# Earlier norms and first products, and one paired comparison on VectorE, in the front of a fused graph and expert kernel

## The chip, the cores and the metric

One core of one Trainium2 chip. The metric is the device time of one execution in microseconds (us). The kernel before takes 1289.39 us, the median of three runs (1287.55 to 1292.88).

## The reference, cut to what matters

Four blocks follow each other on 1250 tokens of 512 numbers: a graph network of three layers, experts, a second graph block with attention, and a last feed-forward block with top-k choices. The change touches only the start of the first:

```
h = _layernorm(x)
for l in range(3):
    neigh = jax.ops.segment_sum(h[src], dst, num_segments=n) * inv_deg
    h = h @ Ws_self[l] + neigh @ Ws_neigh[l] + bs[l]
    if l != 2: h = relu(h)
x = x + h
```

There are 40000 edges (src, dst), sorted by dst.

## The kernel before

The 1250 tokens are 10 tiles of 125. The kernel never gathers rows: it counts the edges into a matrix `adj` (source against target token), and `segment_sum` becomes a matrix product with it. The front, about the first 140 us, builds `adj` and beside it the first layer's products.

**Counting.** The edges lie in 80 *runs* of 4 x 125. For each of the four groups of a run, one matmul of TensorE (line 2397) multiplies a 125 x 125 matrix of ones that marks each edge's source within its tile (`hot_lo`, stationary) by a matrix that marks tile and target (`hot_key`, moving, 80 to 400 columns: 10 tiles times a window of 8 to 40 targets that grows with the run), all in bf16, summed in PSUM. VectorE then adds the window into `adj` (line 1686). Runs 0 to 78 are written out; a small loop does the last one.

Who makes the ones of run t: the first two rows of `hot_lo` (three from run 60 on, where the window is 36 or more; `lo_by_act`) come from ScalarE by a square (line 1050) and a relu for all of them (line 1058). The others come from VectorE, a `tensor_scalar` comparison each (line 1668). `hot_key` is VectorE's: below run `PAIRED` = 60 in one `tensor_tensor` comparison for all four groups (line 1672), on fp16 numbers that lie in pairs (`key_pairs`, `key16`), from run 60 on by four `tensor_scalar` (line 1677). All buffers of ones are double.

**Norms and products.** Beside the runs each tile of x is normed and turned, and the turned tile is multiplied by the layer's two matrices: 80 matmuls of 512 columns in 32 bits (line 2067; each shows as two records), here called products. For tile i: moments on VectorE (line 506, 508), square root on ScalarE (512), reciprocal (516) and normed rows (521) on VectorE, four transposes on TensorE (526), and a copy to `hT` on ScalarE (532). Later ScalarE copies the high part of a tile's neighbour product (line 894, `act_z_hi`, here "z copy") and the self product (938, 939, `act_self`, "self copy"), and VectorE takes the rest (1262, `vec_z`).

**What sets the order.** Each engine has its own program, written out by hand: a loop over a step t, in which `every(t, first, gap)` says that tile i's part stands in step first + gap x i. `FIRST_LN` and `FIRST_Z` are the two starting points, and TensorE issues products up to `products_to(t)`, 8 in 7 runs:

```
def products_to(t):
    return min(max(0, (t - FIRST_Z) * 8 // Z_GAP), 8 * NT - KD)
```

Each engine does its instructions in order. In step t ScalarE makes the squares of run t, then the ones of run t-1, then the norms' and products' parts of step t. VectorE makes the ones and keys of run t, adds run t-2, then its parts. TensorE turns a tile ahead of run t's counts and does products behind them. ScalarE's table of functions must be loaded anew for the square root (once). x comes in two halves by SP's queue (lines 677, 680); the products' weights are line 678.

## Time and profile before

| | us |
|---|---|
| median of 3 runs | 1289.39 |
| the profiled execution, its own time | 1294.25 |
| its span | 1292.5 |
| TensorE busy in the span | 1221.8 |
| VectorE busy | 550.1 |
| ScalarE busy | 452.1 |
| run 0's counts begin | 15.72 |
| the counts of run 78 are added | 139.43 |

The profile is of one execution. A busy TensorE is not TensorE at its peak, since matmuls are pipelined and their ends are modelled; a start is better evidence than an end. In a timeline the bracket behind a row says how long the engine was idle before it and which engine's instruction released it.

### The profile page before, as it was taken

The page shows a single profiled execution, that of the slowest core. Times are in us where ns is not written, and L with a number is a line of the kernel's source. Part 1 is how long each engine was busy: PE and PEld are TensorE (multiplying, and loading weights), DVE is VectorE, ACT ScalarE, POOL GpSimd, SP SyncE. Part 2 cuts the span into 40 slices and gives each one's busy share as a digit, 9 for nine tenths or more (in the row PEclk, how much of TensorE's full clock was granted, in tenths as well). Part 3 has the DMA queues.
Part 4 walks back from the last instruction along what each step waited for, and adds up shares of the span by engine and source line. Part 5 has one row for each costly group of instructions (what it writes and reads, how often), then busy time and mean ns, then how long its engine had stood idle before and what let it go on. Part 6 is the DMA issues. An engine that isn't in the chain of part 4 may idle for free. (4 is left out here: it accounts for less than half of the span.)

```text
span 1292.5 us, 19378 instructions
## 1 busy us (share of the span) xinstructions
PE 1221.8 (95%) x6528; PEld 817.9 (63%) x6529; DVE 550.1 (43%) x1535; ACT 452.1 (35%) x965; POOL 227.9 (18%) x227
## 2 busy tenths in 40 slices
PE   4999899999999899999999999999989999989797
PEld 3555485467458455488787887777465586564465
DVE  8999643333444343100000000001485345675773
ACT  7878533233223300011111111111112343338872
POOL 1000070030000028201111111111453000116530
PEclk9999999999999889999999999999988999999899
DMA  9200000000012300761166114456452000200011
GB/s 225 86 1 1 1 2 1 0 2 2 0 57 82 124 1 1 243 240 49 45 235 247 48 42 167 151 209 231 121 145 87 3 32 2 74 0 1 1 34 48
DMA packets 42978, 98.25 MB, mean 76 GB/s; under 512 B 4142, under 2 KB 6632, under 8 KB 41874
## 3 DMA queue, kind: packets, MB, share of 16 engines
q1 hardware_dynamic: 28642, 68.70, 15.9%
q0 software_dynamic: 6144, 16.45, 4.7%
q10 hardware_dynamic: 8112, 12.08, 2.6%
q8 instruction: 45, 0.74, 0.2%
q14 instruction: 35, 0.29, 0.1%
HBM read 81.02 MB, written 16.17 MB: 75 GB/s over the span
## 5 line engine op out<-in xcount | busy, mean ns | idle before, releaser
L498 PEld LDWEIGHTS psum<-sb_blk,sb_w_reg 128*128 128x128 f32 x1792 | 204.0, 192 | 12.8 <-issue 12.8
L498 PE MATMUL psum<-sb_blk,sb_w_reg 128*128 128x128 f32 x1792 | 205.2, 275 | 1.7 <-issue 1.7
L2145 PE MATMUL psum<-sb_z_reg_r,sb_hT_conv_r 125*125 125x512 f32 x385 | 157.0, 408 | 0.4 <-DVE sb_z_last L1262 0.4
L1434 DVE TENSOR_TENSOR sb_blk<-sb_blk,psum 128x256 f32<-128x256 f32 x56 | 23.6, 421 | 277.0 <-ACT sb_blk L955 277.0
L498 PE MATMUL psum<-sb_hT_conv,sb_w_reg 128*128 128x416 f32 (+3 forms) x336 | 110.0, 485 | 4.8 <-issue 4.8
L2145 PE MATMUL psum<-sb_htok_r,sb_hT_conv_r 125*125 125x512 f32 x285 | 112.9, 396 | 0.0
L2235 PE MATMUL psum<-sb_w_reg,sb_blk 128*128 128x512 f32 x224 | 100.8, 592 | 0.0
L498 PEld LDWEIGHTS psum<-sb_hT_conv,sb_w_reg 128*128 128x128 f32 x336 | 67.2, 204 | 42.2 <-issue 38.2
L2145 PEld LDWEIGHTS psum<-sb_z_reg_r,sb_hT_conv_r 125*125 125x125 f32 x385 | 72.0, 187 | 18.0 <-issue 0.7
L2067 PE MATMUL psum<-sb_w_reg,sb_hT_conv 128*125 128x512 f32 x160 | 81.8, 605 | 0.0
L955 ACT ACTIVATE sb_blk<-psum 128x256 f32<-128x256 f32 x56 | 21.5, 384 | 163.9 <-PE psum L498 163.9
L905 ACT CAST sb_hT_conv_r<-sb_a_reg 125x625 fp32r<-125x625 f32 x80 | 56.2, 717 | 54.7 <-PE psum L2145 50.7
L2397 PEld LDWEIGHTS psum<-sb_hT_conv,sb_sil 125*125 125x125 bf16 x316 | 37.7, 145 | 52.5 <-issue 23.4
L2235 PEld LDWEIGHTS psum<-sb_w_reg,sb_blk 128*128 128x128 f32 x224 | 40.4, 190 | 40.2 <-issue 40.2
L2397 PE MATMUL psum<-sb_hT_conv,sb_sil 125*125 125x80 bf16 (+7 forms) x316 | 49.6, 282 | 14.4 <-ACT sb_sil L1058 7.0
L2145 PEld LDWEIGHTS psum<-sb_htok_r,sb_hT_conv_r 125*125 125x125 f32 x285 | 53.5, 188 | 12.6 <-issue 0.5
L1050 ACT ACTIVATE sb_blk<-sb_sil,sb_blk 125x125 bf16<-125x125 f16 x177 | 59.9, 394 | 1.8 <-DVE sb_blk L1622 0.5
L2118 PE MATMUL psum<-sb_w_reg,sb_hT_conv 128*125 128x512 f32 x120 | 56.4, 592 | 0.0
L959 ACT COPY sb_blk<-psum 128x512 f32<-128x512 f32 x28 | 16.4, 586 | 93.1 <-PE psum L2235 64.4
L779 POOL TENSOR_TENSOR sb_w_reg<-sb_w_reg 128x1024 f32<-128x1024 f32 x2 | 4.8, 2394 | 240.5 <-DVE sb_blk L1276 161.8
L757 POOL COPY sb_blk<-sb_blk 128x1 int32 (+1 forms) x29 | 5.3, 184 | 235.8 <-PE psum L2214 235.8
L831 POOL DMA_INDIRECT slot_tokens<-sb_tok_id,sb_list_i x30 | 36.4, 1214 | 52.1 <-DVE sb_list_i L1864 43.3
(452 smaller groups left out, 2004.7 us busy)
## 6 DMA issues: line engine op xcount, KB each, us to landing
sb_hT_conv<-w_expert SPq DMA_DIRECT2D x7, 2048.0 KB
sb_w_reg<-w_expert SPq DMA_DIRECT2D x6, 2048.0 KB, 18.4
sb_hT_conv<-w_expert SPq DMA_DIRECT2D x7, 1024.0 KB, 12.1
slot_outs<-sb_blk ACTq DMA_DIRECT2D x28, 256.0 KB
sb_w_reg<-w_expert SPq DMA_DIRECT2D x6, 1024.0 KB, 20.3
sb_w_reg<-w_gnn SPq DMA_DIRECT2D x1, 4096.0 KB
sb_w_reg<-w_qkv SPq DMA_DIRECT2D x1, 3072.0 KB, 20.8
slot_outs<-sb_blk ACTq DMA_DIRECT2D x1, 2560.0 KB, 12.8
```

What stands on the lines that cost most here:

```text
L498: ins = e.matmul(out, l, r, start=(n == 0), stop=(n == len(pairs) - 1))
L831: e.indirect_dma_start(list_dram, bass.IndirectOffsetOnAxis(ap=list_i[:, i, k:k + 1], axis=0), tok_id[:, i:i + 1], None).then_inc(list_sca ...
L905: e.copy(counts_at(l, n), adj[:, h * HALF_T:(h + 1) * HALF_T, tile(i)]).then_inc(counts_in, 1)
L955: e.activation(silg[:, h, :], psum[:, 1 + h, 0:HF], ACT.Silu).then_inc(s_sil, 1)
L959: e.copy(y_blk, psum[:, 5, :]).then_inc(s_y, 1)
L1050: e.activation(sq_lo[t % 2][:, j, :], neg_iota, ACT.Square, bias=neg_lo[:, c:c + 1], scale=-1.0).then_inc(lo_squared, 1)
L1434: e.tensor_tensor(hidT[:, 2 * h:2 * h + 2, :].rearrange("p k n -> p (k n)"), silg[:, h, :], psum[:, 1 + h, HF:2 * HF], ALU.mult).then_inc( ...
L2067: ins = e.matmul(psum[0:TP, bank, :], hT[:, k, tile(i)], w_gnn[:, 0 if own else 1, k, :], start=(k == 0), stop=(k == KD - 1))
L2118: ins = e.matmul(psum[0:TP, bank, :], still[:, k, :], moving[:, k, :], start=(first and k == 0), stop=(k == 1), skip_group_check=True)
L2145: ins = e.matmul(psum[0:TP, b, :], counts_at(l, 2 * i + n // NT)[:, s % HALF_T, :], z[s], start=(n == 0), stop=(n == len(pairs) - 1))
L2235: ins = e.matmul(psum[:, 5, :], hidT[:, k, :], w_dn[:, k, :], start=(k == 0), stop=(k == KD - 1))
L2397: ins = e.matmul(psum[0:TP, t % 3, 0:NT * run_win(t)], hot_lo[n][:, j, :], hot_keys(t, j), start=(j == 0), stop=(j == RUN - 1))
```

## The change

Three edits in the front:

1. `FIRST_LN` goes from 2 to 0 and `FIRST_Z` from 8 to 5: norms begin in step 0, products behind run 5, and z copies, self copies and `vec_z` three steps earlier.
2. Closer steps within a tile's norm: the normed rows stand in the step of the reciprocal (`FIRST_LN + 2`, not + 3), the transposes at + 3 (not + 4), ScalarE's copy at + 4 (not + 6).
3. Below run 60, VectorE's two rows of ones are made by one `tensor_tensor` comparison of fp16 pairs: a doubled iota `lo_pairs` against two neighbouring edges' numbers from `lo16`. The result lies interleaved, so that TensorE reads groups 2 and 3 of `hot_lo` with a gap of one element (`hot_los`). Two set-up instructions are added: `lo_pairs` (250 numbers) and `lo16` (320).

```diff
@@ -196,6 +196,10 @@
         key_pairs = z_reg[0:TP, 8 * D:8 * D + PAIR_KEYS].bitcast(FP16).rearrange("p (w b) -> p w b", b=2)
         key16 = z_reg[0:TP, 8 * D + PAIR_KEYS:8 * D + PAIR_KEYS + ECH // 2].bitcast(FP16)
 
+        lo_pairs_at = 8 * D + PAIR_KEYS + ECH // 2
+        lo_pairs = z_reg[0:TP, lo_pairs_at:lo_pairs_at + TP].bitcast(FP16).rearrange("p (n b) -> p n b", b=2)
+        lo16 = z_reg[0:TP, lo_pairs_at + 126:lo_pairs_at + 126 + ECH // 2].bitcast(FP16)
+
         def by_run(v):
             return v.rearrange("p (r j) -> p r j", j=RUN)
         dst_f, neg_lo, key0, key, gap = (blk[0:TP, 1536 + n * ECH:1536 + (n + 1) * ECH] for n in range(5))
@@ -538,6 +542,14 @@
             i, rest = divmod(t - first, gap)
             return [i] if rest == 0 and 0 <= i < NT else []
 
+        def paired_lo(t):
+            return hot_lo[t % 2].rearrange("p j n -> p (j n)")[:, 2 * TP:].rearrange("p (n b) -> p n b", b=2)
+
+        def hot_los(t, j):
+            if t < PAIRED and j >= 2:
+                return paired_lo(t)[:, :, j - 2]
+            return hot_lo[t % 2][:, j, :]
+
         def paired_keys(t):
             return hot_key[t % 2].rearrange("p j n -> p (j n)")[:, 0:RUN * NT * run_win(t)].rearrange(
                 "p (a w b) -> p a w b", a=RUN // 2, b=2)
@@ -596,7 +608,7 @@
 
 
         FIRST_X = NT // 2
-        FIRST_LN, FIRST_Z, Z_GAP = 2, 8, 7
+        FIRST_LN, FIRST_Z, Z_GAP = 0, 5, 7
 
         def of_tiles(t, s, first=0, last=NT):
 
@@ -1059,7 +1071,7 @@
                                  scale=-1.0).then_inc(zeroed_lo_ready, 1)
                 for i in every(t, FIRST_LN + 1, 2):
                     act_std(e, 0, i)
-                for i in every(t, FIRST_LN + 6, 2):
+                for i in every(t, FIRST_LN + 4, 2):
                     e.wait_ge(turned, i + 1)
                     act_turned(e, i, 6 + i % 2)
                 for i in every(t, FIRST_Z + 5, Z_GAP):
@@ -1599,6 +1611,7 @@
             e.wait_ge(v_own, v.n)
             few, many = slice(0, PAIRED * RUN), slice(PAIRED * RUN, ECH)
             e.tensor_tensor(key[:, many], key[:, many], gap[:, many], ALU.add).then_inc(v_own, v.up())
+            e.tensor_copy(lo16, neg_lo).then_inc(v_own, v.up())
             e.tensor_tensor(key16[:, few], key[:, few], gap[:, few], ALU.add).then_inc(edge_vec, 1)
 
         def vector(e):
@@ -1613,6 +1626,8 @@
             e.memset(slot_i, 0).then_inc(v_own, v.up())
             e.memset(a_reg[:, ZERO_POOL:], 0.0).then_inc(v_own, v.up())
 
+            e.wait_ge(edge_pool, IOTAS)
+            e.tensor_copy(lo_pairs, neg_iota.unsqueeze(2).to_broadcast([TP, TP, 2])).then_inc(v_own, v.up())
             e.wait_ge(ld_edges, 32)
             e.tensor_copy(dst_f, dst_i).then_inc(edge_vec, 1)
             e.tensor_scalar(tile_i, src_i, TILE_MUL, None, ALU.mult).then_inc(v_own, v.up())
@@ -1663,9 +1678,13 @@
                     n, w = t % 2, run_win(t)
                     if t >= 2:
                         e.wait_ge(adj_mm, t - 1)
-                    for j in range(lo_by_act(t), RUN):
-                        c = RUN * t + j
-                        e.tensor_scalar(hot_lo[n][:, j, :], neg_iota, neg_lo[:, c:c + 1], None, ALU.is_equal)
+                    if t < PAIRED:
+                        own = lo16[:, RUN * t + 2:RUN * t + 4]
+                        e.tensor_tensor(paired_lo(t), lo_pairs, own.unsqueeze(1).to_broadcast([TP, TP, 2]), ALU.is_equal)
+                    else:
+                        for j in range(lo_by_act(t), RUN):
+                            c = RUN * t + j
+                            e.tensor_scalar(hot_lo[n][:, j, :], neg_iota, neg_lo[:, c:c + 1], None, ALU.is_equal)
                     if t < PAIRED:
                         of_all = [TP, RUN // 2, NT * w, 2]
                         own = key16[:, RUN * t:RUN * (t + 1)].rearrange("p (a b) -> p a b", b=2)
@@ -1693,7 +1712,7 @@
                     vec_moments(e, 0, i)
                 for i in every(t, FIRST_LN + 2, 2):
                     vec_rstd(e, 0, i)
-                for i in every(t, FIRST_LN + 3, 2):
+                for i in every(t, FIRST_LN + 2, 2):
                     if i >= 3:
                         e.wait_ge(turned, i - 2)
                     vec_normed(e, 0, i, htok[:, 7 + i % 3, :])
@@ -2382,7 +2401,7 @@
 
 
             for t in range(STATIC_RUNS):
-                for i in every(t, FIRST_LN + 4, 2):
+                for i in every(t, FIRST_LN + 3, 2):
                     e.wait_ge(ln_out, i + 1)
                     if i >= 2:
                         e.wait_ge(hT_in, i - 1)
@@ -2394,7 +2413,7 @@
                     e.wait_ge(hot_ready, RUN * t + j + 1)
                     if j == 0:
                         e.wait_ge(zeroed_lo_ready, ZEROED + t + 1)
-                    ins = e.matmul(psum[0:TP, t % 3, 0:NT * run_win(t)], hot_lo[n][:, j, :], hot_keys(t, j),
+                    ins = e.matmul(psum[0:TP, t % 3, 0:NT * run_win(t)], hot_los(t, j), hot_keys(t, j),
                                    start=(j == 0), stop=(j == RUN - 1))
                 ins.then_inc(adj_mm, 1)
                 for product in range(products_to(t), products_to(t + 1)):
```

**TensorE, runs 0 to 10**, before. 125x80 and 125x120 are count matmuls, four a run; `sb_ident,sb_htok` are a tile's four transposes; `sb_w_reg,sb_hT_conv` is a product.

```order
L2397 MATMUL psum<-sb_hT_conv,sb_sil 125x80 x24
L526 MATMUL psum<-sb_ident,sb_htok 128x125 x4
L2397 MATMUL psum<-sb_hT_conv,sb_sil 125x80 x8
L526 MATMUL psum<-sb_ident,sb_htok 128x125 x4
L2397 MATMUL psum<-sb_hT_conv,sb_sil 125x80 x4
L2067 MATMUL psum<-sb_w_reg,sb_hT_conv 125x512
L2397 MATMUL psum<-sb_hT_conv,sb_sil 125x80 x4
L2067 MATMUL psum<-sb_w_reg,sb_hT_conv 125x512
L526 MATMUL psum<-sb_ident,sb_htok 128x125 x4
L2397 MATMUL psum<-sb_hT_conv,sb_sil 125x120 x4
```

The same place now (lines of the changed kernel):

```order
L2416 MATMUL psum<-sb_hT_conv,sb_sil 125x80 x12
L530 MATMUL psum<-sb_ident,sb_htok 128x125 x4
L2416 MATMUL psum<-sb_hT_conv,sb_sil 125x80 x8
L530 MATMUL psum<-sb_ident,sb_htok 128x125 x4
L2416 MATMUL psum<-sb_hT_conv,sb_sil 125x80 x4
L2086 MATMUL psum<-sb_w_reg,sb_hT_conv 125x512
L2416 MATMUL psum<-sb_hT_conv,sb_sil 125x80 x4
L2086 MATMUL psum<-sb_w_reg,sb_hT_conv 125x512
L530 MATMUL psum<-sb_ident,sb_htok 128x125 x4
L2416 MATMUL psum<-sb_hT_conv,sb_sil 125x80 x4
L2086 MATMUL psum<-sb_w_reg,sb_hT_conv 125x512
```

The first transposes moved from ahead of run 6 to ahead of run 3, the first product from behind run 8 to behind run 5; tile i's transposes stand ahead of run 3 + 2i, in the runs between a product stands behind each.

**ScalarE, from the squares of runs 0 and 1 on**, before. 125x125 are squares, 125x250 a run's ones; line 512 is the norm's square root, 532 the copy of a turned tile.

```order
L1050 ACTIVATE sb_blk<-sb_sil,sb_blk 125x125 x4
L1058 ACTIVATE sb_sil<-sb_blk 125x250
L1050 ACTIVATE sb_blk<-sb_sil,sb_blk 125x125 x2
L1058 ACTIVATE sb_sil<-sb_blk 125x250
L1050 ACTIVATE sb_blk<-sb_sil,sb_blk 125x125 x2
L1058 ACTIVATE sb_sil<-sb_blk 125x250
L512 ACT_TABLE_LOAD
L512 ACTIVATE sb_rstd<-sb_mv,sb_eps 125x1
```

Now:

```order
L1062 ACTIVATE sb_blk<-sb_sil,sb_blk 125x125 x4
L1070 ACTIVATE sb_sil<-sb_blk 125x250
L516 ACT_TABLE_LOAD
L516 ACTIVATE sb_rstd<-sb_mv,sb_eps 125x1
L1062 ACTIVATE sb_blk<-sb_sil,sb_blk 125x125 x2
L1070 ACTIVATE sb_sil<-sb_blk 125x250
L1062 ACTIVATE sb_blk<-sb_sil,sb_blk 125x125 x2
L1070 ACTIVATE sb_sil<-sb_blk 125x250
L516 ACTIVATE sb_rstd<-sb_mv,sb_eps 125x1
L1062 ACTIVATE sb_blk<-sb_sil,sb_blk 125x125 x2
L1070 ACTIVATE sb_sil<-sb_blk 125x250
L536 COPY sb_hT_conv<-psum 128x4x125
```

The first square root stood behind the ones of runs 0 to 2, and now stands behind those of run 0 alone. The first copy stands behind the ones of run 3 (before, behind those of run 7), so the ones of run 4 come after a copy that waits for transposes ahead of run 3's counts.

## Rows read from the trace of the kernel before

**Rows 1.** Busy us by stretch, after stretch and us: PE, PEld, DVE, ACT, POOL, PEclk
```profile
30.60:45.00 14.40, 14.05 (x81) 8.02 (x80) 14.24 (x57) 12.64 (x40) 0.00 (x0) 1.00 0.70 217
...
120.00:137.80 17.80, 15.30 (x63) 8.57 (x62) 17.07 (x63) 14.36 (x41) 0.00 (x0) 1.00 0.00 0
```

**Rows 2.** Timeline, runs 2 to 5: start us, us, engine line op out<-in [idle before <-releaser]
```profile
16.91 1.28 ACT L512 ACT_TABLE_LOAD   x1
...
17.69 0.69 DVE L506 BATCH_NORM_STATS2 sb_stats<-sb_x_res 125x6 f32<-125x512 f32 x1
...
19.95 0.62 PE L2397 MATMUL psum<-sb_hT_conv,sb_sil 125*125 125x80 bf16 x4 [2.18 <-ACT sb_sil L1058]
...
22.63 0.62 PE L2397 MATMUL psum<-sb_hT_conv,sb_sil 125*125 125x80 bf16 x4 [1.03 <-ACT sb_sil L1058]
```

**Rows 3.** Timeline, runs 6 to 10
```profile
24.10 0.40 DVE L1668 TENSOR_SCALAR sb_sil<-sb_sil,sb_blk 125x125 bf16<-125x125 f16 x2
...
26.96 0.40 DVE L1668 TENSOR_SCALAR sb_sil<-sb_sil,sb_blk 125x125 bf16<-125x125 f16 x2
...
27.26 2.03 PE L2067 MATMUL psum<-sb_w_reg,sb_hT_conv 128*125 128x512 f32 x2
...
29.33 1.10 PE L2067 MATMUL psum<-sb_w_reg,sb_hT_conv 128*125 128x512 f32 x2
...
30.27 0.59 PE L526 MATMUL psum<-sb_ident,sb_htok 125*128 125x125 f32 x4
...
30.70 0.39 PE L2397 MATMUL psum<-sb_hT_conv,sb_sil 125*125 125x120 bf16 x4
```

**Rows 4.** Timeline, ScalarE's copy and ones (runs 13, 14), and runs 22 and 24
```profile
34.63 0.56 ACT L532 COPY sb_hT_conv<-psum 128x500 f32<-128x500 f32 x1
...
35.68 0.40 ACT L1058 ACTIVATE sb_sil<-sb_blk 125x250 bf16<-125x250 bf16 x1
...
49.80 0.49 PE L2397 MATMUL psum<-sb_hT_conv,sb_sil 125*125 125x180 bf16 x4
...
50.00 0.58 ACT L532 COPY sb_hT_conv<-psum 128x500 f32<-128x500 f32 x1 [0.61 <-PE psum L526]
...
52.65 0.49 PE L2397 MATMUL psum<-sb_hT_conv,sb_sil 125*125 125x180 bf16 x4
```

**Rows 5.** Timeline of TensorE, runs of 220 columns, and one after a gap
```profile
62.67 0.56 PE L2397 MATMUL psum<-sb_hT_conv,sb_sil 125*125 125x220 bf16 x4
...
63.06 1.03 PE L2067 MATMUL psum<-sb_w_reg,sb_hT_conv 128*125 128x512 f32 x2
...
63.93 0.56 PE L2397 MATMUL psum<-sb_hT_conv,sb_sil 125*125 125x220 bf16 x4
...
67.01 0.58 PE L2397 MATMUL psum<-sb_hT_conv,sb_sil 125*125 125x220 bf16 x4 [0.39 <-ACT sb_sil L1058]
```

**Rows 6.** Timeline, VectorE in the last runs; the four products behind run 78
```profile
129.26 0.25 DVE L1668 TENSOR_SCALAR sb_sil<-sb_sil,sb_blk 125x125 bf16<-125x125 f16 x1
...
130.84 0.25 DVE L1668 TENSOR_SCALAR sb_sil<-sb_sil,sb_blk 125x125 bf16<-125x125 f16 x1
...
137.96 3.60 PE L2067 MATMUL psum<-sb_w_reg,sb_hT_conv 128*125 128x512 f32 x8
```

**Rows 7.** Single lines: engine op, duration ns min/median/max, first and last start
```profile
L1668 DVE TENSOR_SCALAR sb_sil<-sb_sil,sb_blk x139: 229/250/264, 15.0 to 136.2; 125x125 bf16<-125x125 f16 x139
L1672 DVE TENSOR_TENSOR sb_hT_conv<-sb_z_reg x60: 316/568/820, 15.4 to 104.1; 125x320 bf16<-125x320 f16 x10, 125x480 bf16<-125x480 f16 x10, 125x720 bf16<-125x720 f16 x10, 125x880 bf16<-125x880 f16 x10
L2397 PEld LDWEIGHTS psum<-sb_hT_conv,sb_sil x316: 132/136/231, 15.7 to 137.6; 125*125 125x125 bf16 x158
L2067 PEld LDWEIGHTS psum<-sb_w_reg,sb_hT_conv x160: 185/188/335, 27.2 to 140.5; 128*125 128x125 f32 x160
```

**Rows 8.** DMA of 13 to 15 us; landing of line 678 (weights of the first products)
```profile
DMA packets 54, 0.88 MB, mean 442 GB/s; under 512 B 0, under 2 KB 0, under 8 KB 0
DMA to landing us min/median/max: 17.0/17.0/17.0
```

## The prediction

> **What bounds the kernel now.** I read the busy time by stretch first, then the timelines run by run. The change lies in the front, the first 140 us of 1292.5; all later work starts when the last counts are added. In the norms' stretch TensorE is busy 14.05 of 14.40 us and VectorE 14.24; in the last runs VectorE 17.07 of 17.80 and TensorE 15.30 [rows 1]. Neither share tells who waits, so each kind of run is read by itself. I call "run n begins" the start of its four count matmuls.
>
> - Runs 0 to 9: TensorE waits. Run 3 begins at 19.95 after 2.18 us on ScalarE's ones, run 5 at 22.63 after 1.03 us [rows 2]. VectorE goes from one pair of runs to the next in 26.96 - 24.10 = 2.86 us with no idle time shown [rows 3]: it bounds this stage. The first product takes 2.03 us for its two halves, the next 1.10 [rows 3]: TensorE works until about 29 as at the lower of its two levels (1.2 GHz against 2.4); in the stretch from 30.6 the granted clock is 1.00, the upper one [rows 1].
> - Runs 10 to 24, with norms: begin at 30.70 and 52.65 [rows 3, 4], 21.95 us for 14 runs, 3.1 us a pair.
> - Runs 24 to 59: 63.93 - 62.67 = 1.26 us a run, of it 0.39 counts and 63.93 - 63.06 = 0.87 the product [rows 5]: TensorE goes without a gap. Once in seven runs it waits for ScalarE, 0.39 us shown [rows 5], because ScalarE had waited for the product whose high part it copies.
> - Last runs: VectorE, 130.84 - 129.26 = 1.58 us a run without idle time [rows 6]; TensorE's work of a run is there 0.39 x 400/220 = 0.71 of counts (400 columns, not 220) and 0.87, as much.
>
> **The change, part by part**, made against the profiled execution (1294.25 us outside, span 1292.5; the median of the runs shown is 1289.39, 4.9 lower, and I move the result down by that).
>
> *One comparison for VectorE's two rows.* The two old ones take 250 ns each [rows 7] and are shown as 0.42 together, and the next instruction starts some 0.33 after them. The key comparison has the same form as the new one (16-bit pairs against broadcast pairs): 316 ns for 320 columns up to 820 ns for 1280, 60 instructions [rows 7], so (820-316)/960 = 0.525 ns a column, and 250 columns take 316 - 70 x 0.525 = 0.28 us, 0.20 to the next start. Saved: 0.13 us in each of 60 runs, 7.8 us of VectorE at most. What of it is on the path: only where VectorE bounds. In runs 24 to 59 TensorE has no gap to give but the one in seven, and that ends on ScalarE's ones [rows 5], with VectorE's keys close ahead of them; for five such gaps I take 0.3 us in all. From run 60 on nothing is changed. Bounds: 0 and 7.8.
>
> *Set-up.* The doubled iota lies in VectorE's wait for the edges: 0. The 16-bit copy of 320 numbers stands before the first keys: about 0.3, less the 0.13 of run 0, so run 0 begins 0.2 later.
>
> *Norms from run 0.* x must have landed by about 15.9. Between 13 and 15 us no packet under 8 KB moves [rows 8], and x's rows are 2 KB: it has. VectorE now does the first moments (0.69, [rows 2]) right after run 0's ones, and ScalarE's first square root stands ahead of the ones of run 1 instead of behind those of run 2. The table load of 1.28 us [rows 2] is hidden in that wait, but run 1's ones come only at about 17.9 (moments done 16.65, root 17.0, squares 0.6, ones 0.4). Run 2 then begins near 19.0, the first transposes come before run 3, run 3 at 20.5, run 4 at 22.2, run 5 at 23.5: 0.9 later than before, with two tiles turned instead of none.
>
> *Products from run 5.* Their weights landed at 2.5 + 17.0 = 19.5 [rows 8]. Product 0 starts at about 24 and finds TensorE at the slow rate: two products of about 1.8 [rows 3] instead of 0.87 bring run 7 to 28.4. The three runs that lose a product, 72 to 74, are VectorE's, which goes on at 1.58 without them: gain 0.
>
> *The copy one run closer.* This is the term that decides. Before, ScalarE copies a turned tile in step n+2 for transposes ahead of run n; now in step n+1. From the copy's start to the end of the next ones is 35.68 + 0.40 - 34.63 = 1.45 us (copy, two squares, ones) [rows 4]. The copy starts 50.00 - 49.80 = 0.2 after run n begins [rows 4], so the ones stand at 1.65 and TensorE is there at 0.2 + 0.87 = 1.1. Before, those ones were for run n+2, at 2.2: no wait. Now they are for run n+1: TensorE stands 0.6 each time, unless that run has two products. A z copy (0.5) or a self copy (0.5) in the same step is added. A pair is then 0.2 + 1.45 + 0.06, plus counts 0.2, product 0.87 and transposes 30.70 - 30.27 = 0.43 [rows 3] = 3.2 us. From run 7 (28.4): run 8 at 30.0, run 9 at 31.5, run 10 with z at 33.5, run 12 at 36.9 (two products hide the copy), run 14 with self at 40.6, 16 at 43.8, 18 at 47.2 (z), 20 at 51.3 (two products in run 18), 22 at 54.6, and without norms 24 at 57.0. Before it was 52.65: 4.3 later, though two tiles' transposes (0.86) have moved ahead of run 10. Bounds of this term: 0 if ScalarE keeps ahead, and 4.3 + 1.
>
> *Weight loads.* Two of the four stationary operands are now read with a gap of one element. A load of the packed rows takes 136 ns, the nearest slower one, 32-bit, 188 [rows 7]. Bounds: 0, and 2 x 60 x 0.052 = 6.2 us; I take 0, as the moving operand is already read in this way and runs of 220 columns keep to 0.39 us. The Trainium skill ("TensorE: Matmul & The Clock Gate", Weight-path perf modes) lists fast weight load as reading its chunks packed or strided, but for 128 columns, and these have 125; by its pattern line the sum keeps this 0, by a load that falls back it would have the 6.2. No row here shows a 16-bit load with a gap.
>
> **Sum:** +4.3 at run 24 (the 0.2 and the 0.9 are in it) - 0.3 = +4.0 us. From run 24 on both orders hold the same products for each run, and the end is VectorE's: the shift goes through. 1294.25 + 4.0 = 1298.3 for an execution like the profiled one, 1293.4 for the median. A measurement of this kernel can tell about 0.5% (6.4 us) from no change.
>
> **The rivals.**
> A. *Forecast, 0.45.* 1293.4, own range 1290 to 1297.
> B. *VectorE's pace decides, 0.27.* ScalarE's order makes no wait, since it is busy only 12.64 of 14.40 us [rows 1], and VectorE, with no idle time in runs 3 to 20, gets 2.86 - 0.26 = 2.6 us a pair. For: VectorE's rows follow each other without a gap there [rows 3]. Against: a share of 88% is what an engine has that makes others wait once a pair. Twelve pairs x 0.26 = 3.1 less: 1286.3; all 60 runs, 1281.6.
> C. *Slower loads, 0.10.* The gap in the stationary rows costs 6.2 on TensorE, which bounds runs 24 to 59; on top of A 1299.6. It decides as soon as a load takes longer than its neighbour's matmul (0.10 us at 220 columns, half that at 80). This is the rival on the other side: slower by 0.8%.
> D. *TensorE falls to its slow rate at the end, 0.10.* Runs 72 to 78 have only counts, 0.71 of 1.58 us, where before four such runs stood. The eight half products behind them take 3.60 [rows 6]; at half rate 7.2. At most 3.6, some of it under VectorE's next step; I price 2.6: 1296. Against: the last four runs kept full rate.
> E. *It doesn't do what it says, 0.08.* The new comparison reads its pairs at one column a cycle (0.42, as long as the two), and the norm steps fall into idle time: 1289.4.
>
> **How the numbers follow.** Below 1283 only B's best end: 0.06. Above 1295.8: C, half of D, the tail of A: 0.19. Between: 0.75. The range leaves out C's upper part and B's lower: 1285 to 1299.5.
>
> **What the profile after should show.** The new comparison at about 280 ns x60 (right), over 350 (E). Run 1 beginning near 18 and run 5 near 23.5. ScalarE idle before its copy, waiting for the transposes, in most of ten cases (before, a wait of 0.61 stands at the copy of 50.00 [rows 4], and none at that of 34.63); TensorE waiting for ScalarE's ones some 0.6 us per pair; run 10 near 33.5 and run 24 near 57. Bf16 weight loads still at 136 ns (else C). Half products after run 78 at 590 ns (else D). VectorE 1.58 a run at the end. If run 24 begins before 52.6, the term of the closer copy is wrong, and B or the two tiles turned ahead pay after all.

## The result and the profile after

The changed kernel takes 1293.85 us, median of 20 runs (1289.78 to 1297.72); the kernel before, beside it, 1288.36 (1285.31 to 1292.93, 20 runs). The ratio is 1.0044, 95% interval 1.0035 to 1.0053: 5.5 us slower, less than the 0.5% that the prediction called the smallest difference worth a name, but now certain. Forecast were 4.0 us more. A second set of 12 runs gave 1.0046 (1.0032 to 1.0059).

The profiled execution of the changed kernel took 1292.79 us outside, span 1291.1, and the one before 1294.25. The two differ in the other direction, so neither span can be used for a difference of 5 us: the work behind the front scatters by more. What repeats far better is the position of the front's end. I take the start of the first matmuls that need the finished `adj`, those of the degree row. Before and after:

```profile
145.81 7.02 PE L498 MATMUL psum<-sb_a_reg,sb_ones_tp_b 125*1 125x418 bf16 x30 [0.77 <-DVE sb_a_reg L1738]
```

```profile
151.76 6.97 PE L502 MATMUL psum<-sb_a_reg,sb_ones_tp_b 125*1 125x418 bf16 x30 [0.77 <-DVE sb_a_reg L1757]
```

The front ends 5.95 us later. This position is called the *front's end* below; in the second trace of the changed kernel it is 151.83.

**Where the 6 us are.** The busy time by stretch of the changed kernel (columns as in [rows 1]):

```profile
30.60:45.00 14.40, 11.87 (x64) 6.34 (x63) 12.14 (x40) 10.71 (x35) 0.00 (x0) 1.00 0.68 216
45.00:60.00 15.00, 13.13 (x68) 6.95 (x68) 11.60 (x36) 11.64 (x36) 0.00 (x0) 1.00 0.03 8
...
120.00:137.80 17.80, 15.33 (x60) 8.36 (x59) 17.08 (x66) 15.21 (x45) 0.00 (x0) 1.00 0.00 1
```

From 30.6 to 45 all three engines have fallen together: TensorE from 14.05 to 11.87, VectorE from 14.24 to 12.14, ScalarE from 12.64 to 10.71 [rows 1]. When every engine does less in the same time, none of them is the bound; they wait for each other in a ring. The last runs are as they were: 17.08 against 17.07 of VectorE.

The ring can be read in the timeline of one pair, runs 15 and 16 (only rows of the ring):

```profile
42.67 0.59 PE L530 MATMUL psum<-sb_ident,sb_htok 125*128 125x125 f32 x4
...
43.10 0.39 PE L2416 MATMUL psum<-sb_hT_conv,sb_sil 125*125 125x120 bf16 x4
...
43.30 0.58 ACT L536 COPY sb_hT_conv<-psum 128x500 f32<-128x500 f32 x1 [0.89 <-PE psum L530]
...
43.78 0.69 ACT L1062 ACTIVATE sb_blk<-sb_sil,sb_blk 125x125 bf16<-125x125 f16 x2
...
44.37 0.40 ACT L1070 ACTIVATE sb_sil<-sb_blk 125x250 bf16<-125x250 bf16 x1
...
44.91 0.42 PE L2416 MATMUL psum<-sb_hT_conv,sb_sil 125*125 125x120 bf16 x4 [0.50 <-ACT sb_sil L1070]
```

TensorE turns a tile (42.67) and counts run 15 (43.10). ScalarE had stood 0.89 us for those transposes; only at 43.30 does it copy, then it squares (43.78) and makes the ones (44.37), and with these run 16 begins at 44.91, after TensorE stood 0.50. The copy starts 0.20 after run 15, and the ones end 1.67 after it: the prediction had 0.2 and 1.65. The groups of the two lines say how regular this is. ScalarE's copy between 15 and 60 us (first the line with min, median and max in ns, then the idle time before it, us and times), and VectorE's comparison over all its 60 runs:

```profile
L536 ACT COPY sb_hT_conv<-psum x10: 577/578/579, 20.2 to 54.4; 128x500 f32<-128x500 f32 x10
its engine sat idle before it (us, times) until:
  PE psum L530: 10.3, 10
```

```profile
L1683 DVE TENSOR_TENSOR sb_sil<-sb_z_reg x60: 256/290/292, 14.9 to 109.7; 125x250 bf16<-125x250 f16 x60
its engine sat idle before it (us, times) until:
  PE psum L2416: 8.9, 14
```

All ten copies now wait for their transposes, 10.3 us together. The new comparison takes 290 ns (forecast: 280), and VectorE stands 8.9 us in front of it, waiting for TensorE to release a buffer of ones.

### The profile page after: what moved, and what is told of

The parts are those of the page before. It is cut to its first block and busy times, and to the rows that moved or that the text cites. A ratio compares the mean times of both kernels' runs of the same rounds, so it can differ in the third digit from the quotient of the medians.

```text
span 1291.1 us, 19320 instructions
## 1 busy us (share of the span) xinstructions
PE 1218.3 (94%) x6528; PEld 814.2 (63%) x6529; DVE 546.0 (42%) x1477; ACT 451.7 (35%) x965; POOL 227.2 (18%) x227
## 5 line engine op out<-in xcount | busy, mean ns | idle before, releaser
L2416 PE MATMUL psum<-sb_hT_conv,sb_sil 125*125 125x80 bf16 (+7 forms) x316 | 49.4, 281 | 18.6 <-ACT sb_sil L1070 10.2
L2137 PE MATMUL psum<-sb_w_reg 128*125 128x512 f32 x96 | 44.3, 594 | 1.3 <-ACT sb_sil L921 1.3
```

Source lines behind the costliest of these rows:

```text
L2137: ins = e.matmul(psum[0:TP, bank, :], still[:, k, :], moving[:, k, :], start=(first and k == 0), stop=(k == 1), skip_group_check=True)
L2416: ins = e.matmul(psum[0:TP, t % 3, 0:NT * run_win(t)], hot_los(t, j), hot_keys(t, j), start=(j == 0), stop=(j == RUN - 1))
```

## The experiments

All times are medians, taken in five sets with the kernel before beside them in each. The level differs from set to set (the kernel before took 1288.4, 1293.6, 1295.4, 1294.7 and 1287.8 us), so only ratios are compared. The trace gives four positions: where runs 0, 10 and 24 begin (run 24 is the first one after the last tile is turned), and the front's end. Run 0 itself scatters: in the six traces of kernels that are alike up to there (both traces of the changed kernel, copy + 6, copy + 5, and the two changed ones with the z copy later) it begins between 15.52 and 16.36 us. Positions of two kernels can differ by as much without a cause in the edit, so stretches, from run 0, from run 10 or from run 24 on, are better evidence than positions.

| kernel | run 0 | run 10 | run 24 | front's end | ratio to before (95%) |
|---|---|---|---|---|---|
| before | 15.72 | 30.70 | 52.65 | 145.81 | 1 |
| changed | 15.52 | 33.98 | 59.08 | 151.76 | 1.0044 (1.0035 to 1.0053) |
| changed, again | 15.62 | 34.04 | 59.14 | 151.83 | 1.0046 (1.0032 to 1.0059) |
| changed, copy + 6 | 16.04 | 31.91 | 53.94 | 147.10 | 1.0010 (0.9994 to 1.0027) |
| changed, copy + 5 | 15.92 | 31.69 | 54.09 | 146.88 | 1.0008 (0.9989 to 1.0027) |
| before, copy + 5 | 15.43 | 31.44 | 57.42 | 151.42 | 1.0035 (1.0016 to 1.0053) |
| before, comparison alone | 15.60 | 32.07 | 53.69 | 147.62 | 0.9999 (0.9982 to 1.0015) |
| before, shift alone | 15.77 | 32.27 | 54.46 | 147.15 | 1.0013 (0.9995 to 1.0030) |
| changed, comparison undone | 16.15 | 33.08 | 58.15 | 151.03 | 1.0049 (1.0026 to 1.0072) |
| changed, copy + 6, z copy later | 16.32 | 32.38 | 53.99 | 143.39 | 0.9972 (0.9956 to 0.9988) |
| changed, z copy later | 16.36 | 34.15 | 59.14 | 148.33 | 1.0005 (0.9986 to 1.0024) |
| before, z copy later | 15.66 | 31.23 | 53.60 | 142.57 | 0.9974 (0.9956 to 0.9991) |
| before, z and self copy later | 15.74 | 30.94 | 53.32 | 142.07 | 0.9976 (0.9961 to 0.9991) |
| before, z copy later, comparison | 15.65 | 31.89 | 53.76 | 142.72 | 0.9968 (0.9953 to 0.9984) |

### Is it the closer copy?

Four kernels in one set. The first takes the change and moves ScalarE's copy alone back:

```diff
-                for i in every(t, FIRST_LN + 4, 2):
+                for i in every(t, FIRST_LN + 6, 2):
                     e.wait_ge(turned, i + 1)
```

> The changed kernel with ScalarE's copy of a turned tile two steps later again (+6 as before); all else of the change stays. Theory A (the closer copy makes TensorE wait for ScalarE's ones, eight or nine times 0.6 us and more where a z or self copy joins it): TensorE's waits for ScalarE's ones between runs 7 and 22 go, run 24 begins near 54.5 instead of 59.1, and the small loop's counts begin 4 to 5 us earlier than 149.43; time about 1289 to 1290. Rival S (the earlier start itself costs it: square root ahead of run 1, cold products): run 24 still begins after 58, time stays at about 1293.

Measured: front's end 147.10, run 24 at 53.94 instead of 59.08. 4.66 of the 5.95 us are back (from run 0 on, 5.2 of 6.15; some 0.8 of that is TensorE's slow rate, which lasted longer in the trace of the change, see the last section), and the ratio is 1.0010 with an interval that holds 1. TensorE's waits for ScalarE's ones fall from 10.2 us to 4.4.

The second does the reverse, the closer copy and nothing else in the kernel before:

```diff
-                for i in every(t, FIRST_LN + 6, 2):
+                for i in every(t, FIRST_LN + 5, 2):
                     e.wait_ge(turned, i + 1)
```

> The kernel before with nothing changed but ScalarE's copy one step earlier (FIRST_LN + 5 instead of + 6), so that it comes one run behind its transposes. Theory A: TensorE waits about 0.6 us in seven or eight of the ten pairs; run 24 begins near 56.5 instead of 52.65, the small loop's counts near 147.3 instead of 143.47; time about 1292 (+3.5 to +4.5). Rival S: nothing changes by more than 1 us.

Measured: front's end 151.42, 5.6 us later (forecast 3.5 to 4.5), and ratio 1.0035. Its copies wait as those of the whole change do:

```profile
L532 ACT COPY sb_hT_conv<-psum x10: 558/578/579, 24.1 to 57.6; 128x500 f32<-128x500 f32 x10
its engine sat idle before it (us, times) until:
  PE psum L526: 7.7, 9
```

Removed, most of the loss goes; done alone, the loss comes. This step is shown from both sides.

The third and fourth make the two other parts alone. The comparison (edit 3 of the change without edits 1 and 2):

```diff
+                    if t < PAIRED:
+                        own = lo16[:, RUN * t + 2:RUN * t + 4]
+                        e.tensor_tensor(paired_lo(t), lo_pairs, own.unsqueeze(1).to_broadcast([TP, TP, 2]), ALU.is_equal)
```

> The kernel before with the paired comparison alone (lo_pairs, lo16, one tensor_tensor, the interleaved stationary rows); all steps as before. Theory A (VectorE's 0.13 us a run lies beside other work): run 24 begins within 0.7 us of 52.65, the small loop's counts between 142.7 and 143.6; time 1288 +-1. Rival V (VectorE's pace bounds runs 0 to 24 and the norms' pairs): run 24 begins 3 us earlier, the small loop 3 to 7 us earlier, time 1281 to 1285.

The shift (edit 1 alone):

```diff
-        FIRST_LN, FIRST_Z, Z_GAP = 2, 8, 7
+        FIRST_LN, FIRST_Z, Z_GAP = 0, 5, 7
```

> The kernel before with FIRST_LN = 0 and FIRST_Z = 5 alone (norms from run 0, products from run 5; distances within a tile's norm and both comparisons as before). Theory A (the earlier start costs about a microsecond at the beginning, cold products included, and two tiles turned ahead give about as much back): run 10 near 32.5, run 24 near 53.7, small loop within 1.5 us of 143.47; time 1287.5 to 1290.5. Rival S (the shift itself is the loss): run 24 after 56, the small loop after 147, time above 1292.

Measured: ratios 0.9999 and 1.0013, both with intervals that hold 1, so neither is a gain or a loss that these runs can tell. In the traces the front ends 1.81 and 1.34 us later; for the comparison alone I had expected 0.1 us at most. For both, nearly all of it lies before run 10 (1.37 and 1.57), where products meet TensorE at its slow rate; the last section returns to that. VectorE's saving does not appear in the time: in the third kernel it stood 6.7 us before the new comparison.

### How far must the copy stand?

With + 6 the copy stood three steps behind the transposes, with + 4 one. The kernel before had two:

```diff
-                for i in every(t, FIRST_LN + 4, 2):
+                for i in every(t, FIRST_LN + 5, 2):
                     e.wait_ge(turned, i + 1)
```

> The changed kernel with ScalarE's copy at FIRST_LN + 5, two steps behind the step of the transposes, which is the distance of the kernel before (the earlier run had + 6, three steps). Theory A (the distance to the transposes decides, and two steps are enough): ScalarE's idle time before its copies under 1 us, small loop's counts at 144.3 to 145.2, as with + 6. Rival (the wait shrinks by degrees, and each step gives back a part): half of it left, loop at about 147.

Measured: front's end 146.88, the copies wait once:

```profile
L536 ACT COPY sb_hT_conv<-psum x10: 551/558/577, 21.9 to 50.2; 128x500 f32<-128x500 f32 x10
its engine sat idle before it (us, times) until:
  PE psum L530: 0.4, 1
```

One step is the whole difference between 10.3 and 0.4 us of waiting. Over these three positions it works as a threshold, not by degrees. With + 4, when the transposes ahead of run n end, only run n's ones are there, so TensorE has one run in hand, some 1.1 us, and ScalarE needs 1.65 until the next ones. With + 5 the ones of run n + 1 are there as well, and two runs in hand are longer than 1.65. The closer normed rows and transposes of edit 2 were not made alone; they are still in the kernels with the copy at + 5 and + 6, and these cannot be told from before.

### Does the comparison matter inside the change?

The comparison's trace when it was made alone pointed to a loss, the arithmetic to a gain. So it was taken out of the change (`lo_pairs`, `lo16` and the gapped `hot_los`, too):

```diff
-                    if t < PAIRED:
-                        own = lo16[:, RUN * t + 2:RUN * t + 4]
-                        e.tensor_tensor(paired_lo(t), lo_pairs, own.unsqueeze(1).to_broadcast([TP, TP, 2]), ALU.is_equal)
-                    else:
-                        for j in range(lo_by_act(t), RUN):
+                    for j in range(lo_by_act(t), RUN):
```

> The changed kernel with the comparison undone: VectorE's two rows of ones by two comparisons as before, everything else as changed. Theory A (VectorE has idle time at run n already, so what one comparison saves only lengthens it): VectorE's idle time before its rows shrinks from about 8.9 us to 2 or 3, small loop's counts at 149.0 to 150.2 (after: 149.43), time equal to after within 1 us. Rival B' (VectorE's 0.13 us a run is on the path although it waits): loop at 153 or later, time 4 us above after. Rival C' (the comparison costs, as the 1.8 us by which its loop came late when it was made alone seems to say): loop at 147.6, time 1.8 us under after.

Measured: ratio 1.0049 (the change: 1.0044 and 1.0046), front's end 151.03. From run 10 to the front's end it takes 117.95 us, and with the comparison 117.78: VectorE works 0.13 us less in each of 50 runs and 0.17 us arrive. VectorE's idle time before its rows is 6.8 us instead of 8.9; the expectation of 2 to 3 was too low, as the wait is mostly TensorE's standing still, not VectorE's speed. The other 0.9 us lie before run 10: run 0 began 0.63 us later in this trace, and from run 0 to run 10 it took 16.93 us against 18.46. Up to run 5 the two are alike (7.58 and 7.56); behind it the rate comes in again, as the second product took 1.10 here, not 2.05. The loop's counts were expected no more than 0.4 us earlier and came 0.95 earlier (148.48); the whole time shows nothing of it.

### The second wait of the same kind

In the trace before, TensorE stood once in seven runs, 0.39 us ahead of run 34 [rows 5]. The cause proposed here is the same one. The z product of a tile ends behind run `FIRST_Z + 3`, and ScalarE's z copy stands in step `FIRST_Z + 5`: then the ones of run `FIRST_Z + 4` are the last ones made, and TensorE has that one run in hand, 1.26 us [rows 5] against 1.65. The difference is the 0.39. (The gaps ahead of the other tiles' runs are not all of this size, see below.) ScalarE's z copies before (all ten):

```profile
L894 ACT CAST sb_z_reg_r<-psum x10: 567/586/587, 33.3 to 133.2; 125x512 fp32r<-125x512 f32 x10
its engine sat idle before it (us, times) until:
  PE psum L2067: 11.0, 8
```

The prediction took that wait as given. If the reason is right, one step more should bring a kernel that is faster than both. The edit, in the kernel before and in the change with its copy at + 6:

```diff
-                for i in every(t, FIRST_Z + 5, Z_GAP):
+                for i in every(t, FIRST_Z + 6, Z_GAP):
                     act_z_hi(e, 0, i, z_bank(0, i))
...
-                for i in every(t, FIRST_Z + 6, Z_GAP):
+                for i in every(t, FIRST_Z + 7, Z_GAP):
                     vec_z(e, 0, i, z_bank(0, i), z_lo_rows)
```

> The kernel before, with nothing changed but ScalarE's copy of z at FIRST_Z + 6 (not + 5) and VectorE's low part at FIRST_Z + 7. Theory A: the 0.39 us that TensorE waits once in seven runs goes: about eight times 0.4, so the small loop's counts begin at about 140.5 against 143.47, and the time falls by 2 to 3 us (ratio 0.998). Rival V (VectorE bounds from run 60 on and takes it back): loop within 0.5 us of 143.5, ratio 1.000.

> The changed kernel with the copy of the turned tile at FIRST_LN + 6 (as in the run before this) and, besides, ScalarE's copy of z at FIRST_Z + 6 (not + 5) and VectorE's low part at FIRST_Z + 7. Theory A (an engine that works in order must not meet a wait for the product that TensorE has only just issued; the z copy, too, stands one step too close, and costs TensorE about 0.5 us for each of the tiles copied before run 60, some seven): no wait of ScalarE before the z copies, TensorE's waits for ScalarE's ones down from 4.4 us to under 1, run 24 at about 53.0, the small loop's counts at about 142 against 144.76; time 2 to 3 us under the kernel with the copy alone moved back, so 1292 on a chip where before takes 1293.6. Rival V (VectorE's pace sets the last 20 runs and takes back what TensorE gains before): the waits vanish but the loop begins within 0.5 us of 144.8.

Measured: front's end 142.57 and 143.39, 3.2 and 3.7 us earlier than without the edit; ratios 0.9974 and 0.9972, both intervals wholly below 1. It is the first gain in this study, some 3.5 us; the loop's counts came 0.5 and 1.2 us earlier than expected. In the second kernel TensorE's waits for ScalarE's ones fell to 2.6 us, not under 1: 2.1 of them lie before run 5. The stretch from 60 to 90 us before, and with the z copy later:

```profile
60.00:90.00 30.00, 29.02 (x129) 16.34 (x128) 27.43 (x82) 22.95 (x69) 0.00 (x0) 1.00 0.00 1
```

```profile
60.00:90.00 30.00, 30.00 (x133) 17.32 (x132) 28.67 (x87) 24.39 (x72) 0.00 (x0) 1.00 0.00 1
```

TensorE goes without any gap there, and the waits before the z copies fall to:

```profile
L894 ACT CAST sb_z_reg_r<-psum x10: 562/582/587, 35.1 to 130.1; 125x512 fp32r<-125x512 f32 x10
its engine sat idle before it (us, times) until:
  PE psum L2067: 1.6, 4
```

The rival, that VectorE's last 20 runs take the gain back, is refuted: runs 60 to 72 take 19.52 us instead of 21.03. The gaps add up to more than 0.39 each. From run 24 on TensorE stood 0.22 to 0.58 us ahead of each of runs 27, 34, 41, 48, 55, 62, 69 and 77, and longest ahead of run 76, 4.7 us together:

```profile
135.17 0.86 PE L2397 MATMUL psum<-sb_hT_conv,sb_sil 125*125 125x400 bf16 x4 [1.37 <-DVE sb_hT_conv L1677]
```

With the edit one gap of 0.69 us is left, ahead of run 77. The trace puts runs 27, 48, 69 and 76 down to VectorE's keys or adds, not to ScalarE's ones. The edit moves `vec_z` along with the z copy, and the two were not moved apart, so how much each gave is not shown; that the place of this pair of steps cost the 3.5 us is shown, in two kernels.

Is the z wait another loss than the copy's, or the same one twice? The edit was made in the change with its close copy left in place:

> The changed kernel with the z copy alone moved one step later (FIRST_Z + 6, low part + 7); the copy of the turned tile stays one step behind the transposes (FIRST_LN + 4). Theory A (two separate waits that add): the z waits go, some 3.5 us as in the kernel before, while the copy's waits stay until run 24: run 10 at about 33.4, run 24 at 57.5 to 58.5, degree-row matmuls at about 148.0 against 151.76, VectorE still with 6 us or more of idle time before its comparison. Rival (the two waits are one: whichever is taken away, the other takes its place): matmuls within 1 us of 151.8.

Measured: front's end 148.33 (expected 148.0), ratio 1.0005. The two waits add. But run 24 begins at 59.14, not before 58.5 as I expected. Run 0 began 0.84 us later in this trace; from run 0 to run 24 it is 42.78 us against 43.56, so little was gained up to there. While tiles are turned, TensorE waits for the ones behind the tile's copy anyway, and for the second tile the later z copy falls into the same step as a copy of a turned tile: run 10 now stands 0.50 us instead of 0.98, and run 18 0.98 instead of 0.50. After run 24 only the z copies are left, and moving them gains 3.5 us here (92.68 to 89.19 from run 24 to the end) and 4.2 in the kernel before (93.16 to 88.97), where the edit's trace had lost 1 us up to run 24, about half of it to the slow rate.

Next, whether every wait inside ScalarE costs. Its self copy waits as well, and could move too:

```diff
-                for i in every(t, FIRST_Z + 9, Z_GAP):
+                for i in every(t, FIRST_Z + 10, Z_GAP):
                     if i < NT - 1:
                         act_self(e, i)
```

> The kernel before with the z copy at FIRST_Z + 6 and the low part at + 7 (the previous run), and besides ScalarE's copy of the tile's own product at FIRST_Z + 10 instead of + 9. ScalarE is seen to wait 0.57 us for the product before this copy as well, as long as it did before the z copy. Theory A (a wait inside ScalarE costs only what is left of it when its next ones are due, and the own copy's wait shows no gap on TensorE in the trace): nothing gained, first next matmuls (the ones of the degree row) at 142.5 as with the z copy alone, time the same within 1 us. Rival (every wait of ScalarE for a fresh product costs TensorE): another 3 us, matmuls at 139.5.

Measured: front's end 142.07, ratio 0.9976; from run 24 to the end 88.75 us against 88.97. TensorE gained 0.2 us at most. Before this edit ScalarE's waits ahead of its self copies were

```profile
L938 ACT COPY sb_hT_conv<-psum x10: 557/578/583, 40.5 to 137.6; 125x500 f32<-125x500 f32 x10
its engine sat idle before it (us, times) until:
  PE psum L2067: 11.9, 8
```

and with the edit only the last was left, 5.23 us behind run 78. The seven that went had 0.38 to 1.25 us each, 6.7 together; the eight before the z copies had 0.89 to 1.82, 11.0 together. So waits of about a microsecond are dear at one place and free at the other, and the count of runs in hand says which: a self product ends behind run `FIRST_Z + 6`, its copy stands in step `FIRST_Z + 9`, so that TensorE has two runs in hand when the wait ends (some 2.5 us against 1.65). The z copy had one. This count agrees with what became of each of the three kinds of copy when it was moved; it is a reading of the order and the traces, and no run varied the work in hand by itself.

Last, the comparison where it has its best chance, with ScalarE's waits gone:

> The kernel before with the z copy one step later and the comparison of pairs, no shift and no closer copy: the candidate that holds both savings. Theory A (TensorE has no gap from run 12 to about 110 us once the z copy is later, and VectorE is never more than two runs ahead, so its saving before run 60 can't be kept for the last runs): degree-row matmuls at 142.6 within 0.5 us (+1 if the rate of TensorE rises a product later), ratio to before 0.997, as without the comparison. Rival B' (with ScalarE's waits gone VectorE is the bound, and now the comparison pays): matmuls at 140 or earlier, ratio 0.995.

Measured: front's end 142.72, ratio 0.9968 (0.9953 to 0.9984), the lowest of the study, yet within the intervals of 0.9972, 0.9974 and 0.9976. The comparison adds nothing that can be told apart. From run 24 on it is 88.96 against 88.97 us.

### How much is chance?

> The changed kernel once more, with nothing edited: how much of its front is one execution's chance. Theory A (the moment at which TensorE's rate doubles, between 26 and 31.5 us in the kernels so far, even between kernels that are alike up to there, is not set by the instructions): run 10 begins anywhere between 32.5 and 34.2, by how far the second product is still at the slow rate, but from run 10 to the degree row's matmuls it takes 117.8 us within 0.3, as in the first trace. Rival (the order of the instructions fixes the moment): run 10 at 33.98 less or more what run 0 is early or late. The ratio to before: 1.004 again, within 0.002.

Measured: run 10 at 34.04, front's end 151.83, ratio 1.0046. From run 10 on it is 117.79 us, as in the first trace (117.78). In this one repeat the rival was right for what lies before: the second product was slow again (2.05), run 0 began 0.10 us later and run 10 0.06. For one and the same kernel the two traces there are agree to 0.01 us from run 10 on, so differences of a few tenths behind run 10 are read as real here.

## Why the prediction was right, and where it was not

It was right in sign and cause, and near in size: +4.0 us forecast, +5.5 measured. That 1293.4 forecast and 1293.85 measured lie only 0.4 apart is partly luck: the kernel before came out 1.0 us lower than the median used, and the loss 1.5 higher. By its steps:

- *The copy one run closer* was the deciding term. Made alone it moved the front's end by 5.6, undone it gave back 4.66. The 4.3 that the prediction books under it is not its own price but the whole lateness at run 24, with the early start and the slow products in it; the walk was already 2.9 us late at run 7. Measured were 6.43 at run 24, of which 5.14 go when the copy alone is moved back. ScalarE waits in ten of ten copies, and TensorE stands 0.50 us ahead of each of runs 8, 16, 18 and 20 (forecast 0.6), not at all ahead of run 12, as forecast, and twice as long where a z copy or a self copy joins in:

```profile
33.98 0.42 PE L2416 MATMUL psum<-sb_hT_conv,sb_sil 125*125 125x120 bf16 x4 [0.98 <-ACT sb_sil L1070]
...
41.51 0.42 PE L2416 MATMUL psum<-sb_hT_conv,sb_sil 125*125 125x120 bf16 x4 [1.04 <-ACT sb_sil L1070]
```

- *The step that failed in size* is the walk from run 10 (forecast 33.5) to run 24 (57.0); measured 33.98 and 59.08. Of the 2.1 us too few, 0.5 were there at run 10 (at run 7 it was 28.4 forecast, 28.29 measured). Runs 10 to 22 took 22.05 us instead of 21.1, some 0.2 more in each pair: from run 15 to 16 it is 1.81 us (0.2 + 1.45 + 0.06 = 1.71 in the prediction), from 16 to 17 it is 1.59 (1.50). The hand-overs between the engines were counted a tenth of a microsecond too short each. The last 0.65 are the end: I had let runs 22 and 23 run free since no tile is turned there, and forgot the z copy of step 24. It waits 0.55 us for its product, and TensorE has a gap of 0.44 before run 24. With the z copy one step later that gap is gone, and runs 22 to 24 take 2.44 us, not 3.05:

```profile
57.46 0.59 ACT L906 CAST sb_z_reg_r<-psum 125x512 fp32r<-125x512 f32 x1 [0.55 <-PE psum L2086]
```

- *Run 1 and run 5* were forecast near 18 and 23.5. They came at 17.64 and 23.08. The table load was hidden as forecast: it starts at 9.43, long before the first moments are there. Run 0 was forecast 0.2 us later and began 0.20 and 0.10 earlier in the two traces, less than its own scatter. The first two products were priced at 1.8 us each, and TensorE's next instructions start 1.84 us behind each (the transposes at 27.55 behind the second):

```profile
23.48 2.05 PE L2086 MATMUL psum<-sb_w_reg,sb_hT_conv 128*125 128x512 f32 x2
25.32 0.59 PE L2416 MATMUL psum<-sb_hT_conv,sb_sil 125*125 125x80 bf16 x4
25.71 2.05 PE L2086 MATMUL psum<-sb_w_reg,sb_hT_conv 128*125 128x512 f32 x2
...
28.29 0.37 PE L2416 MATMUL psum<-sb_hT_conv,sb_sil 125*125 125x80 bf16 x4
28.49 1.10 PE L2086 MATMUL psum<-sb_w_reg,sb_hT_conv 128*125 128x512 f32 x2
```

- *One comparison for two rows*: 290 ns against the forecast 280. Of the 0.3 us that I put on the path, 0.17 arrived at most. The bound of 7.8 was never near.
- *From run 24 on the shift goes through*: 92.68 us to the front's end, 93.16 before; 0.5 came back. That the end is VectorE's alone was too strong, though: runs 60 to 72 took 21.03 us before and 19.52 with the z copy later. Runs 73 to 77, without products, follow each other in 1.42 us, not in the 1.58 of the forecast.
- *Rival B* (VectorE's pace decides, 0.27) fell. VectorE stood 8.9 us before its comparison. Its argument for, that VectorE's rows follow each other without a gap [rows 3], was a reading of the stretch before run 10, and even there it gave no pace: with the comparison alone run 9 begins 13.60 us behind run 0, before 13.39.
- *Rival C* (slower loads with a gap, 0.10) fell. The loads in all 79 runs have the same minimum, median and maximum as before [rows 7]:

```profile
L2416 PEld LDWEIGHTS psum<-sb_hT_conv,sb_sil x316: 132/136/231, 15.5 to 143.4; 125*125 125x125 bf16 x158
```

  Taken alone, the loads of groups 2 and 3 of runs 0 to 59, the ones with a gap, have medians of 136 and 136.5 ns, and 135 and 133 before. A stationary operand of 16 bits read with a gap of one element costs nothing that shows here. This agrees with the pattern line that the Trainium skill gives for its fast weight load ("TensorE: Matmul & The Clock Gate", Weight-path perf modes: chunks of columns, packed or strided). The Trainium skill ties that load to 128 columns there, and whether loads of 125 are of the fast kind at all, with a gap or without, no run here shows.
- *Rival D* (slow rate at the end, 0.10) fell: the eight half products behind run 78 take 3.60 us, as in [rows 6], although runs 72 to 78 had no product.

```profile
143.59 3.60 PE L2086 MATMUL psum<-sb_w_reg,sb_hT_conv 128*125 128x512 f32 x8
```

- *Rival E* (the comparison as long as the two) fell by the 290 ns.
- What the prediction did not see is the larger lesson: it noted the gap of 0.39 us once in seven runs [rows 5], named its cause, and left it. It is the same fault as the one the change adds, and one step more for the z copy and `vec_z` gave 3.5 us.

The best kernels of the study do not need the change: the kernel before with its z copy one step later runs at 0.9974 of before, and with the comparison at 0.9968, two values that cannot be told apart.

## What to carry to other kernels

Where each engine works through a list in order, a step between producer and consumer is not judged by whether the consumer waits, but by how much work the others have in hand when that wait ends; set against it the waiting instruction and all that is queued behind it up to the next hand-over (here copy, squares and ones, 1.65 us, against one run of 1.1 to 1.26). In this front half a microsecond of wait in an engine that is busy only 74 to 88% of the time stopped the whole ring, and a step later cost nothing. And look at small gaps that come at a fixed interval: some of 0.2 to 0.6 us every seven runs were worth more than a comparison that took a tenth of a microsecond off each of 60.

## What the runs showed of the hardware that was not expected

TensorE's rate doubles once in the front, from a run's four 80-column matmuls in 0.59 to 0.62 us to 0.37 to 0.40, and from a product in 2.05 to 1.10, that is from its level of 1.2 GHz to that of 2.4. The granted clock reads 1.00 in stretches before the rise too (in the changed kernel also from 15.7 to 22 us alone), so that column does not show it; the durations do:

```profile
15.70:30.60 14.90, 11.27 (x55) 7.76 (x55) 11.92 (x45) 10.40 (x34) 0.00 (x0) 1.00 1.07 226
```

The rise does not come at a fixed time. In the changed kernel it was during the transposes that start at 27.55 (27.66 in its second trace), in the one with the comparison undone by 25.82, and in both kernels with the comparison and the old steps at about 31. Three kernels are alike up to run 10, and there the second product took 1.10 (before), 1.55 (z copy later) and 1.17 us (self copy later). The second of these:

```profile
29.41 1.55 PE L2067 MATMUL psum<-sb_w_reg,sb_hT_conv 128*125 128x512 f32 x2
```

That moves run 10 from 30.70 to 31.23, a scatter of 0.5 us in kernels that do the same up to there. The kernels with the comparison, alone and with the later z copy, have run 10 at 32.07 and 31.89, so for them the slow second product (2.05 and 2.00) may be no accident, and it may cost them the 0.7 to 1.4 us that they are behind at run 10. Why one and not the other gets the faster rate early is open; no run here was made to tell it apart. It bounds what any edit of the first ten runs can be seen to do in one trace.
